# An attention-and-experts block on one core: its middle stage written anew, with input summed in place and other orders of loads and stores

## The chip, the cores and the metric

One Trainium2 chip, one of its cores. The time is device microseconds (us) of one execution of the whole program, the median of three runs; it holds the launch's own device work beside the span that the profile shows. A measurement of this kernel tells changes of about 0.3% from none.

## The reference

Input x is 8 sequences of 1024 tokens of width 256. In float32:

```
x = x + attention(layernorm(x))          # 16 heads of width 16, rotary, keys = values
                                         # out @ Wout + bout
y = layernorm(x)
scores = softmax(y @ gate_w.T)           # 8 experts
vals, idx = top_k(scores.T, 1024)        # each expert takes 1024 of the 8192 tokens
z = layernorm(y[idx]) * ln_w + ln_b
h = gelu(z @ fc1.T + b1);  o = (h @ fc2.T + b2) * vals
x = x + (y with o added at the rows idx)
```

## The kernel before, in words

The program has five stages, and three of them stand in one block of instructions (`project_attend_finish`, L1867): *project* (layer norm, the projections, rotary), *attend* (64 pairs of heads), and *finish*. Behind it come *choose* (L1297, the top-k by counting) and *experts* (L1451), each in a block of its own; all engines meet at the end of a block before the next begins. The change is to finish, and to where its first and last transfers stand.

Finish (L869) goes over 64 tiles of 128 tokens, eight to a sequence, two sequences to a pass of 16 tiles. Per tile, with the tile index counted from 0:

- PE multiplies the attended rows by Wout (`project_tile`, L1228) in two chunks of 128 rows, and adds the bias by a third product of a few bfloat16 rows (L1238), into one of two banks of PSUM.
- DVE adds the tile of x (`residual`, L1055) into a buffer of its own, `x2`, takes its mean and variance (`statistics`, L1065; POOL takes the inverse root, L1022), and writes the normalised tile `xf` (L1076). It does the statistics of `xf` as well, for the second layer norm.
- The value that goes to `out` is x2 + xf (`base`: POOL for three tiles in four at L1035, DVE for the fourth at L1084).
- PE turns `xf` round (`turn`, L1240), ACT copies it (L1169), PE multiplies it by the gate weights (`logits`, L1248). Here the gate weights (8 columns) are the stationary operand and 128 tokens stream, so the logits come with experts in rows. For each group of four tiles ACT copies them (`turned_logits`, L1186) and PE turns them back by four products with the identity (`turn_back`, L1261).
- ACT writes the row of the token table (`normalise_again`, L1176); DVE and ACT do the softmax once per sequence (`centre`, `exponential`, `share`, `scores`).

Each engine runs a table of lags: in step j it does stage S for tile j - lag (L877), 16 steps to a pass. The first two passes are written out, the next two are a loop, and a tail follows.

The loads and stores of finish are all issued by SP, in one order that is written by hand (`sync`, L980). SP waits in order, so a load that waits for an engine holds back every store behind it. Its body, per pass:

```
load_o(it + 1, 0)                 # waits until PE is done with that half of o
store_tab(it - 1, 0); store_out(it - 1, 1)
load_x(it + 1, 0)
load_o(it + 1, 1)                 # the same wait, for the other half
store_tab(it - 1, 1); store_out(it, 0)
load_x(it + 1, 1)
```

`x2` holds two sequences, so `residual` of a sequence waits until the store of the sequence two before has landed (L1061). `load_o` waits also for the attended rows on their way to DRAM (`attended`, L583), of all sequences once past the first pass.

The last pairs of attend are not complete when finish begins: the reciprocals and products of the last two pairs are done between the tiles of finish (`invert_last` at DVE's step 6, `scale_second` at POOL's step 6, `scale_last` at its step 12; L1900, L1913). SP issues finish's constants and its first loads (`load_first`, L971) within attend's last pairs (L646). The constants are used by DVE at the start of finish: it splits the bias into three bfloat16 parts (`split_bias`, L1116), and PE waits for that (L1286).

At the end of finish SP waits for all stores (L1017 to L1019), and with it every engine at the end of the block. Choose then loads its four constants (L1346).

Of the kernel before, what the change touches and what calls it, by code (L numbers as in the profile page):

```python
# [868 lines left out]
def finish(nc, ctx, own, x, on_dram, w_out, b_out, w_gate, ident_d, table, out, gate):  # L869


    SEQS = 2
    STEP = SEQS * TILES
    PASSES = B // SEQS
# [16 lines left out]
    o = mem.sb("f_o", [P, SEQS, DC, N])  # L891
    xb = mem.sb("f_x", [P, STEP, D])
    x2 = mem.sb("f_x2", [P, STEP, D])
    xf = mem.sb("f_xf", [P, STEP, D])
    tab = mem.sb("f_tab", [P, STEP, ROW])
    stats = mem.sb("f_stats", [P, 2, STEP, 6])
    mv = mem.sb("f_mv", [P, 2, STEP, 2])
    veps = mem.sb("f_veps", [P, 2, STEP])
    rstd = mem.sb("f_rstd", [P, 2, STEP])
    shift = mem.sb("f_shift", [P, STEP])  # L900
    xfT = mem.sb("f_xfT", [P, 2, DC, P])
    lT = mem.sb("f_lT", [E, 2, LGROUP * P])
# [5 lines left out]
    ps_y = mem.ps("f_ps_y", [P, 2, 512])  # L908
    ps_xT = mem.ps("f_ps_xT", [P, 2, 4, P])
    ps_lT = mem.ps("f_ps_lT", [P, 2, LGROUP * P])  # L910
    ps_l = mem.ps("f_ps_l", [P, 2, 512])

    consts_in = a.sem("f_consts_in")
    set_up = a.sem("f_set_up")
    o_in = [a.sem(f"f_o_in{s}") for s in range(SEQS)]
    x_in = [a.sem(f"f_x_in{s}") for s in range(SEQS)]
    out_out = [a.sem(f"f_out_out{s}") for s in range(SEQS)]
    tab_out = [a.sem(f"f_tab_out{s}") for s in range(SEQS)]
    bias_done = a.sem("f_bias_done")
# [11 lines left out]
    lT_done = a.sem("f_lT_done")  # L931
    back_done = a.sem("f_back_done")
# [16 lines left out]
    flow = Flow(STEP, PASSES)  # L949

    def one(v):
        return bass.ds(v, 1)

    def tiles_of(s):
        return slice(s * TILES, (s + 1) * TILES)

    def load_o(sp, attended, it, s):
        if past(it):

            sp.wait_ge(y_done, it * STEP + (s + 1 - SEQS) * TILES)  # L960
        attended(sp, B if past(it) else s + 1)
        sp.dma_start(o[:, s], o_v[one(it * SEQS + s)].rearrange("o p c n -> p (o c) n")).then_inc(o_in[s], 16)

    def load_x(sp, it, s):
        if past(it):

            sp.wait_ge(x2_done, it * STEP + (s + 1 - SEQS) * TILES)
        sp.dma_start(xb[:, tiles_of(s)], x_v[one(it * SEQS + s)].rearrange("o p i d -> p (o i) d")
                     ).then_inc(x_in[s], 16)

    def load_first(sp, attended):  # L971
        sp.dma_start(bo[:], b_out.rearrange("(o n) -> o n", o=1).to_broadcast([PARTS, D])).then_inc(consts_in, 16)
        sp.dma_start(ident[:], ident_d).then_inc(consts_in, 16)
        sp.dma_start(w[:], w_out.rearrange("(c p) n -> p c n", p=P)).then_inc(consts_in, 16)
        sp.dma_start(wg[:], w_gate).then_inc(consts_in, 16)
        for s in range(SEQS):
            load_o(sp, attended, 0, s)
            load_x(sp, 0, s)

    def sync(sp, attended):  # L980
# [13 lines left out]
        def body(it):  # L994

            load_o(sp, attended, it + 1, 0)
            if past(it):
                store_tab(it - 1, 0)
                store_out(it - 1, 1)
# [994 lines left out]
```

## Time and profile before

| | us |
|---|---|
| median of three runs | 2326.22 |
| lowest, highest | 2322.04, 2328.96 |
| the profiled execution's own time | 2336.65 |
| its span in the profile | 2333.8 |
| finish, first product to last share of the softmax | 1603.97 to 1818.47 |
| waits of DVE's residual in finish for a store to land | 51.3, in 5 waits |

Whole-span busy time: PE 2072.6 (89%), DVE 1951.5 (84%), ACT 1511.4 (65%), POOL 648.8 (28%). Read it with care: these are averages over five stages, and finish is 9% of the span. Engine names: PE is TensorE, PEld its weight loads, DVE VectorE, ACT ScalarE, POOL GpSimd, SP the queue that issues transfers. "Granted clock" is TensorE's, as a share of full speed. In the timeline a row is a start, a duration (of several instructions together where it says x2 or more), the engine, the line, what is written from what, and in brackets how long the engine sat idle before it and what released it.

### The profile page before, as it was taken

How to read it: one execution, taken by the hardware profiler on the slowest of the kernel's cores; microseconds unless marked ns; L12 is line 12 of the kernel's file. 1: busy time of each engine (PE TensorE's matmuls, PEld its weight loads, DVE VectorE, ACT ScalarE, POOL GpSimd, SP SyncE). 2: the span in 40 equal slices, each digit the busy share in tenths (PEclk: the TensorE clock that was granted, in tenths of full speed). 3: DMA queues.
4: the chain of work that ended last, by engine and by line, in shares of the span. 5: the costliest groups of instructions: out<-in, count | busy, mean ns of one | idle time of the engine just before them, and what ended most of it. 6: DMA issues, size and time to landing. Idle time of an engine off the chain costs nothing. (4 is left out here: it accounts for less than half of the span.)

```text
span 2333.8 us, 53856 instructions
## 1 busy us (share of the span) xinstructions
PE 2072.6 (89%) x16812; PEld 1055.1 (45%) x16812; DVE 1951.5 (84%) x3220; ACT 1511.4 (65%) x2858; POOL 648.8 (28%) x864
## 2 busy tenths in 40 slices
PE   6777699999999999999999999999768218999998
PEld 3334233333333333333333333334445117998997
DVE  7888789999999999999999999994546667988864
ACT  3444278888888888888888888884223103455433
POOL 7788101110111110111111011112435013655553
PEclk9999589999999999999999999999879558999999
DMA  3667624444334344333444434433444122343342
GB/s 96 217 222 201 185 54 82 80 81 80 77 73 78 81 79 82 76 74 75 82 79 82 78 75 74 80 67 120 155 146 145 59 74 72 83 101 84 86 83 29
DMA packets 152669, 224.66 MB, mean 96 GB/s; under 512 B 34855, under 2 KB 105098, under 8 KB 152586
## 3 DMA queue, kind: packets, MB, share of 16 engines
q1 hardware_dynamic: 140262, 206.61, 36.7%
q0 software_dynamic: 12288, 17.05, 4.4%
q8 instruction: 38, 0.62, 0.1%
q14 instruction: 45, 0.37, 0.1%
q10 hardware_dynamic: 36, 0.02, 0.0%
HBM read 129.45 MB, written 93.06 MB: 95 GB/s over the span
## 5 line engine op out<-in xcount | busy, mean ns | idle before, releaser
L761 DVE TENSOR_REDUCE a_mx<-a_sm 128x2 f32<-128x1024 f32 x1024 | 1235.6, 1224 | 70.1 <-PE a_sm L709 54.2
L836 ACT ACTIVATE a_prob<-a_st 128x512 f32<-128x512 f32 x2048 | 1113.6, 597 | 180.0 <-PE a_st L672 149.2
L709 PE MATMUL a_sm<-a_k,a_q 48*128 48x512 f32 x2048 | 759.2, 460 | 9.3 <-DVE a_mx L761 7.6
L672 PE MATMUL a_st<-a_q,a_k 50*128 50x512 f32 x2048 | 761.2, 452 | 5.8 <-DMA a_q<-a_mrow 5.8
L696 PE MATMUL a_pv<-a_prob,a_v 128*32 128x256 f32 x8192 | 660.7, 394 | 23.0 <-ACT a_oraw L843 22.4
L672 PEld LDWEIGHTS a_st<-a_q,a_k 50*128 50x128 f32 x2048 | 312.8, 187 | 415.1 <-ACT a_prob L836 395.5
L696 PEld LDWEIGHTS a_pv<-a_prob,a_v 128*32 128x32 f32 x8192 | 162.2, 108 | 404.9 <-issue 198.5
L811 POOL TENSOR_TENSOR a_v<-a_v_raw,a_zero 128x256 f32<-128x256 f32 x64 | 39.7, 622 | 1049.1 <-DMA a_v_raw<-values 900.6
L709 PEld LDWEIGHTS a_sm<-a_k,a_q 48*128 48x128 f32 x2048 | 306.3, 189 | 21.2 <-DVE a_mx L761 19.2
L1779 ACT ACTIVATE e_hT<-e_ps_h,e_b1b 128x512 f32<-128x512 f32 x128 | 88.3, 690 | 213.3 <-PE e_ps_h L1816 203.0
L1816 PE MATMUL e_ps_o<-e_w_high,e_hT_high 128*128 128x256 f32 x512 | 146.9, 287 | 2.8 <-DVE e_biased L1681 2.8
L1816 PE MATMUL e_ps_o<-e_w_low,e_hT_high 128*128 128x256 f32 x512 | 145.4, 284 | 0.0
L1816 PE MATMUL e_ps_o<-e_w_high,e_hT_low 128*128 128x256 f32 x512 | 145.3, 284 | 0.0
L381 PE MATMUL p_ps_q<-p_w,p_xnT 128*128 128x512 f32 x256 | 127.0, 620 | 0.0
L1732 POOL TENSOR_TENSOR e_ahead<-e_row_no 128x1 f32<-128x1 f32 x72 | 49.6, 689 | 266.9 <-DVE e_idx L1625 173.5
L1669 DVE TENSOR_TENSOR e_hT_low<-e_hT,e_hT_high 128x512 fp32r<-128x512 f32 x128 | 86.8, 692 | 42.9 <-ACT e_hT_high L1785 38.5
L1755 POOL DMA_INDIRECT out_dram<-e_ob,e_idx x64 | 110.0, 1719 | 13.7 <-issue 8.4
L1816 PE MATMUL e_ps_h<-e_yT_high,e_w_high 128*128 128x512 f32 x256 | 101.8, 398 | 0.4 <-ACT e_hT L1779 0.4
L1816 PE MATMUL e_ps_h<-e_yT_low,e_w_high 128*128 128x512 f32 x256 | 100.9, 394 | 0.0
L1816 PE MATMUL e_ps_h<-e_yT_high,e_w_low 128*128 128x512 f32 x256 | 100.7, 393 | 0.0
L1816 PEld LDWEIGHTS e_ps_o<-e_w_high,e_hT_high 128*128 128x128 f32 x512 | 98.8, 193 | 3.4 <-DVE e_biased L1681 3.0
L307 POOL TENSOR_TENSOR p_tsin<-p_qkv,p_sin 128x256 f32<-128x256 f32 x128 | 98.3, 788 | 3.7 <-ACT p_qkv L345 3.7
(148 smaller groups left out, 2354.0 us busy)
## 6 DMA issues: line engine op xcount, KB each, us to landing
qkv_parts<-p_parts SPq DMA_DIRECT2D x64, 512.0 KB
a_q<-qkv_parts SPq DMA_DIRECT2D x128, 128.0 KB, 3.5
a_k<-qkv_parts SPq DMA_DIRECT2D x128, 128.0 KB, 4.3
attended<-a_oraw SPq DMA_DIRECT2D x64, 256.0 KB, 3.8
e_w<-in_fc_dram SPq DMA_DIRECT2D x16, 1024.0 KB, 5.4
token_table<-f_tab SPq DMA_DIRECT2D x8, 1056.0 KB, 7.1
p_x<-in_x_dram SPq DMA_DIRECT2D x16, 512.0 KB, 8.1
values<-p_values SPq DMA_DIRECT2D x8, 1024.0 KB, 19.6
```

The lines of the kernel that those rows point to most:

```text
L307: nc.gpsimd.tensor_tensor(ts[:, :, h * HALF:(h + 1) * HALF], src[:, :, (1 - h) * HALF:(2 - h) * HALF], sinb[:, i:i + 1, h * HALF:(h + 1) * ...
L381: mm = nc.tensor.matmul(ps_q[:, k % 2], xnT[:, k % 2, c], w[:, c], start=(c == 0), stop=(c == DC - 1))
L672: nc.tensor.matmul(st[:, slot % RING], kb[rows, q.buf, jt * P:(jt + 1) * P], qb[rows, q.buf, ic * CHUNK:(ic + 1) * CHUNK], start=True, sto ...
L696: mm = nc.tensor.matmul(pv[row:row + 2 * DH, cols], vb[:, q.buf, jt, h, :], prob[:, jt % 2, h, start:start + QUARTER], start=(jt == 0 and ...
L709: mm = nc.tensor.matmul(sm[:, slot, h], qb[rows, q.buf, qt * P:(qt + 1) * P], kb[rows, q.buf, kc * CHUNK:(kc + 1) * CHUNK], start=True, st ...
L761: nc.vector.tensor_reduce(mx[:, qt, kc, :], sm[:, slot], AX.X, ALU.max, negate=True).then_inc(max_done, 1)
L836: nc.scalar.activation(prob[:, jt % 2, h, ic * CHUNK:(ic + 1) * CHUNK], st[:, slot % RING], ACT.Exp, scale=DH ** -0.5).then_inc(drained, 1)
L1669: nc.vector.tensor_tensor(group_of(hT_low, g), hT[:, g % 4], group_of(hT_high, g), ALU.subtract).then_inc(hT_low_done, 1)
L1732: nc.gpsimd.tensor_tensor(ahead[:], row_no[:], row_no[:], ALU.add).then_inc(ahead_done, 1)
L1755: nc.gpsimd.indirect_dma_start(out=out_rows, out_offset=bass.IndirectOffsetOnAxis(ap=idx[:, k, i:i + 1], axis=0), in_=ob[:, i], in_offset= ...
L1779: nc.scalar.activation(hT[:, g % 4], ps_h[:, g % 3], ACT.Gelu_apprx_tanh, bias=b1b[:, k, g % FC:g % FC + 1]).then_inc(gelu_done, 1)
L1816: return nc.tensor.matmul(to, weights, moving, start=first, stop=last)
```

## The change

Finish is written out for all 64 tiles, without a loop, in a new form:

- `xb` holds four sequences instead of two, and `residual` and `base` write into it: `x2` is gone. `load_x` of sequence s waits for the store of sequence s - 4.
- `residual` waits for no store. PE has three banks for the output product instead of two.
- SP's order per sequence s: load o of s + 2, store the table of s - 1, load x of s + 3, store out of s. `load_first` loads x of four sequences instead of two. `load_o` of sequence s waits for the attended rows of sequences up to s only. The last sequence's stores go in halves.
- The logits: 128 tokens are the stationary operand, the 8 columns of the gate weights stream. The result has tokens in rows; `turned_logits`, `turn_back` and their banks are gone.
- The bias product uses all 128 rows: `ones` and `bo_rows` have 128 partitions, rows 3 to 127 of `bo_rows` are zero.
- The constants of finish are loaded and the bias split ahead of project's work (`Early`); Wout and the gate weights are loaded between project and attend.
- SP's waits for the stores of finish stand in the block of choose, behind the loads of its constants (`finished`).
- All lags are three less: the late steps go from 6, 6, 12 to 3, 3, 9, the same tiles as before.

```diff
-    PROJ, STAT, NORM, TURN, LOGITS, SHIFT, NORM2, BACK, CENTRE, SHARE = 3, 4, 7, 8, 9, 10, 11, 11, 12, 13
+    STAT, NORM, TURN, LOGITS, SHIFT, NORM2, CENTRE, SHARE = 1, 4, 5, 6, 7, 8, 9, 10
...
+    OSEQS, XSEQS, TSEQS = 2, 4, 2
+    YBANKS = 3
...
+        self.bo_rows = mem.sb("f_bo_rows", [P, D], BF16)
+        self.ones = mem.sb("f_ones", [P, P], BF16)
...
+    def load_o(sp, attended, s):
+        if s >= OSEQS:
+
+            sp.wait_ge(y_done, (s + 1 - OSEQS) * TILES)
+        attended(sp, s + 1)
+        sp.dma_start(o[:, s % OSEQS], o_v[s]).then_inc(o_in[s % OSEQS], 16)
+
+    def load_x(sp, s):
+        if s >= XSEQS:
+
+            sp.wait_ge(out_out[s % XSEQS], 16 * (s // XSEQS))
+        sp.dma_start(xb[:, ring(s, XSEQS)], x_v[s]).then_inc(x_in[s % XSEQS], 16)
...
+        for s in range(B):
+            if s + OSEQS < B:
+                load_o(sp, attended, s + OSEQS)
+            if s > 0:
+                store_tab(s - 1, 0, s * TILES)
+            if XSEQS <= s + XSEQS - 1 < B:
+                load_x(sp, s + XSEQS - 1)
+            if s < B - 1:
+                store_out(s, 0, (s + 1) * TILES)
...
-                if past(it):
-
-                    dve.wait_ge(out_out[s], 16 * it)
             dve.wait_ge(y_done, n + 1)
-            nc.vector.tensor_tensor(x2[:, k], ps_y[:, k % 2, 0:D], xb[:, k], ALU.add).then_inc(x2_done, 1)
+            nc.vector.tensor_tensor(xb[:, n % XRING], ps_y[:, n % YBANKS, 0:D], xb[:, n % XRING], ALU.add
+                                    ).then_inc(x2_done, 1)
...
-                mm = nc.tensor.matmul(ps_lT[0:E, (k // LGROUP) % 2, i * P:(i + 1) * P], wg[:, c], xfT[:, k % 2, c],
+                mm = nc.tensor.matmul(ps_l[:, s % 2, i * E:(i + 1) * E], xfT[:, n % 2, c], wg[:, c],
                                       start=(c == 0), stop=(c == DC - 1))
...
             for buf, name in ((ident, "ident"), (same, "same"), (before, "before"), (bits, "bits")):
                 sp.dma_start(buf[:], consts[name]).then_inc(consts_in, 16)
+            finished(sp)
...
+            early.load_bias(sp, t["b_out"], t["ident"])
             first.sync(sp, load_pairs)
+            early.load(sp, t["w_out"], t["w_gate"])
             second.sync(sp, stored, load_finish)
...
         def _(dve):
+            early.split_bias(dve)
             first.vector(dve)
             second.vector(dve)
-            third.vector(dve, {6: invert_last})
+            third.vector(dve, {3: invert_last})
```

PE's instructions for tiles in the middle of finish, before: output product, bias, turn, logits, and every fourth tile the turn back.

```order
L1236 MATMUL f_ps_y<-f_w,f_o 128x256 x2
L1238 MATMUL f_ps_y<-f_bo_rows,f_ones 128x256
L1245 MATMUL f_ps_xT<-f_ident,f_xf 128x128 x2
L1257 MATMUL f_ps_lT<-f_xfT,f_wg 8x128 x2
L1270 MATMUL f_ps_l<-f_ident,f_lT 128x8 x4
```

And of the change, at the same place:

```order
L1231 MATMUL f_ps_y<-f_w,f_o 128x256 x2
L1233 MATMUL f_ps_y<-f_bo_rows,f_ones 128x256
L1240 MATMUL f_ps_xT<-f_ident,f_xf 128x128 x2
L1251 MATMUL f_ps_l<-f_wg,f_xfT 128x8 x2
L1231 MATMUL f_ps_y<-f_w,f_o 128x256 x2
```

The logits product writes 128 rows of 8 instead of 8 rows of 128, and the four products of the turn back are gone.

SP's queue within attend's last pairs, before (`a_den`, `a_num` are the denominators and numerators that come back for a pair, L612 the store of its reciprocals):

```order
L607 DMA a_num<-attended 64x1x512
L972 DMA f_bo<-in_b_out_dram 3x256
L973 DMA f_ident<-in_ident_dram 128x128
L974 DMA f_w<-in_w_out_dram 128x2x256
L975 DMA f_wg<-in_w_gate_dram 128x16
L962 DMA f_o<-attended_normalised 128x2x1024
L968 DMA f_x<-in_x_dram 128x8x256
L962 DMA f_o<-attended_normalised 128x2x1024
L968 DMA f_x<-in_x_dram 128x8x256
L612 DMA reciprocal_denominators<-a_rden 128x16
```

And of the change:

```order
L607 DMA a_num<-attended 64x1x512
L1002 DMA f_o<-attended_normalised 128x2x1024
L1008 DMA f_x<-in_x_dram 128x8x256
L1002 DMA f_o<-attended_normalised 128x2x1024
L1008 DMA f_x<-in_x_dram 128x8x256 x3
L612 DMA reciprocal_denominators<-a_rden 128x16
```

Four small loads are gone from here, and two loads of x (1 MB each) have come in front of L612.

## Rows read from the trace of the kernel before

**Rows 1.** Busy time in stretches: us, engines' busy (count), granted clock, DMA share, GB/s.

```profile
1776.00:1804.00 28.00, 28.00 (x153) 17.16 (x152) 21.00 (x93) 12.07 (x29) 17.24 (x32) 1.00 0.37 126
...
1827.00:1890.00 63.00, 11.31 (x39) 9.44 (x40) 44.63 (x146) 0.00 (x0) 0.00 (x0) 0.50 0.00 0
```

**Rows 2.** Waits of 1550 to 1950 us: who waited, for whom, total us, times, longest.

```profile
DVE f_x L1063 <- DMA out_dram<-f_x: 51.3, 5, 11.5
```

**Rows 3.** Timeline, DVE, residual of tiles 3, 48 and 63: start, us, instruction, idle before.

```profile
1612.13 0.42 DVE L1063 TENSOR_TENSOR f_x<-f_ps_y,f_x 128x256 f32<-128x256 f32 x1
...
1768.70 0.42 DVE L1063 TENSOR_TENSOR f_x<-f_ps_y,f_x 128x256 f32<-128x256 f32 x1 [10.89 <-DMA out_dram<-f_x]
...
1805.51 0.42 DVE L1063 TENSOR_TENSOR f_x<-f_ps_y,f_x 128x256 f32<-128x256 f32 x1 [0.17 <-PE f_ps_y L1238]
```

**Rows 4.** Timeline, PE, one tile at full clock and the group's turn back behind it.

```profile
1755.03 1.13 PE L1236 MATMUL f_ps_y<-f_w,f_o 128*128 128x256 f32 x4
...
1756.09 0.28 PE L1238 MATMUL f_ps_y<-f_bo_rows,f_ones 3*128 3x256 bf16 x1
...
1756.30 0.44 PE L1245 MATMUL f_ps_xT<-f_ident,f_xf 128*128 128x128 f32 x2
...
1756.66 0.60 PE L1257 MATMUL f_ps_lT<-f_xfT,f_wg 128*8 128x128 f32 x4
...
1757.20 1.05 PE L1270 MATMUL f_ps_l<-f_ident,f_lT 8*128 8x8 f32 x8
...
1758.18 1.13 PE L1236 MATMUL f_ps_y<-f_w,f_o 128*128 128x256 f32 x4
```

**Rows 5.** Timeline, DVE, residuals of tiles 8, 10 and 50.

```profile
1620.77 0.42 DVE L1063 TENSOR_TENSOR f_x<-f_ps_y,f_x 128x256 f32<-128x256 f32 x1 [0.83 <-PE f_ps_y L1238]
...
1625.05 0.42 DVE L1063 TENSOR_TENSOR f_x<-f_ps_y,f_x 128x256 f32<-128x256 f32 x1 [0.60 <-PE f_ps_y L1238]
...
1774.16 0.42 DVE L1063 TENSOR_TENSOR f_x<-f_ps_y,f_x 128x256 f32<-128x256 f32 x1 [0.37 <-PE f_ps_y L1238]
```

**Rows 6.** Timeline, SP queue, the store of sequence 4.

```profile
1758.17 0.40 SPq L984 DMA_DIRECT2D out_dram<-f_x  x1
```

**Rows 7.** Busy time in three-microsecond stretches, columns as in rows 1.

```profile
1637.00:1640.00 3.00, 3.00 (x20) 2.06 (x18) 1.31 (x4) 1.14 (x3) 2.16 (x4) 1.00 1.02 237
...
1763.00:1766.00 3.00, 0.00 (x0) 0.00 (x0) 0.00 (x0) 0.00 (x0) 0.00 (x0) 0.67 1.09 361
```

**Rows 8.** Timeline, PE, the output product just after a stall.

```profile
1744.04 2.08 PE L1236 MATMUL f_ps_y<-f_w,f_o 128*128 128x256 f32 x4
```

**Rows 9.** Timeline, SP queue, from attention's last pairs to the finish.

```profile
1578.07 0.47 SPq L972 DMA_DIRECT2D f_bo<-in_b_out_dram  x1
...
1583.66 4.21 SPq L612 DMA_DIRECT2D reciprocal_denominators<-a_rden  x1
...
1595.63 0.60 SPq L616 DMA_DIRECT2D a_rrep<-reciprocal_denominators  x1
...
1603.85 0.60 SPq L605 DMA_DIRECT2D a_den<-attended  x1
```

**Rows 10.** Timeline, DVE and PE at the same place.

```profile
1599.50 0.25 DVE L563 RECIPROCAL a_rden<-a_den 128x16 f32<-128x16 f32 x1 [20.31 <-DMA a_den<-attended]
...
1603.97 2.05 PE L1236 MATMUL f_ps_y<-f_w,f_o 128*128 128x256 f32 x4 [4.24 <-DVE f_bo_rows L1131]
```

**Rows 11.** Timeline, from the last logits to the choice of tokens.

```profile
1815.25 0.56 ACT L1192 COPY f_lT<-f_ps_lT 8x512 f32<-8x512 f32 x1
...
1816.96 0.23 DVE L1100 TENSOR_REDUCE f_lmax<-f_ps_l 128x8 f32<-128x64 f32 x1 [1.13 <-PE f_ps_l L1270]
...
1818.87 0.37 SPq L991 DMA_DIRECT2D token_table<-f_tab  x1
...
1827.39 1.12 PE L1355 MATMUL c_ps_t<-c_ident,c_by_group 128*128 128x128 f32 x4 [10.47 <-DMA c_bits<-in_bits_dram]
```

**Rows 12.** Timeline, DVE, the program's first statistics.

```profile
6.86 1.41 DVE L231 BATCH_NORM_STATS2 p_stats<-p_x 128x6 f32<-128x256 f32 x4 [5.94 <-DMA p_sin<-in_rot_sin_dram]
```

More of the change, by code:

```diff
@@ new lines, in steps, with tile, ring @@
+    def steps(body, last_lag):
+        for j in range(TILES_ALL + last_lag):
+            body(j)
+    def tile(j, lag):
+        return j - lag if 0 <= j - lag < TILES_ALL else None
+    def ring(s, seqs):
+        return slice((s % seqs) * TILES, (s % seqs + 1) * TILES)
+    def load_o(sp, attended, s):
[7 more added lines that the diff above has]
+        sp.dma_start(xb[:, ring(s, XSEQS)], x_v[s]).then_inc(x_in[s % XSEQS], 16)
@@ L1220, in body @@
+        def body(j):
+            n = tile(j, TURN)
+            if n is not None:
+                turned(n)
+            n = tile(j, NORM2)
+            if n is not None:
+                normalise_again(n)
             for stage, lag in ((exponential, CENTRE), (scores, SHARE)):
-                tile = flow.at(it, j, lag)
-                if tile and tile[1] % TILES == TILES - 1:
-                    stage(*tile)
-        flow.run(act, body, SHARE)
+                n = tile(j, lag)
+                if n is not None and n % TILES == TILES - 1:
+                    stage(n // TILES)
@@ L1274, in body @@
-        def body(it, j):
-            for stage, lag in ((project_tile, PROJ), (turn, TURN), (logits, LOGITS)):
-                tile = flow.at(it, j, lag)
-                if tile:
-                    stage(*tile)
-            tile = flow.at(it, j, BACK)
-            if tile and tile[1] % LGROUP == LGROUP - 1:
-                turn_back(*tile)
-        banks_left(pe)
-        pe.wait_ge(consts_in, 64)
-        pe.wait_ge(set_up, 3)
-        pe.wait_ge(bias_done, 3 * PARTS)
-        flow.run(pe, body, BACK)
@@ L1289, in finish, with body @@
-    return Stage(sync, tensor, vector, scalar, gpsimd), load_first
+        def body(j):
+            for stage, lag in ((project_tile, 0), (turn, TURN), (logits, LOGITS)):
+                n = tile(j, lag)
+                if n is not None:
+                    stage(n)
+        banks_left(pe)
+        pe.wait_ge(early.consts_in, 32)
+        pe.wait_ge(early.bias_done, 3 * PARTS)
+        steps(body, LOGITS)
+    return Stage(sync, tensor, vector, scalar, gpsimd), load_first, stored
 ROUNDS = 15
@@ L1294, with choose @@
 UNROLL = 5
[L1297 removed]
+def choose(nc, gate, consts, places_hi, places_lo, finished):
     GROUP = TOK // 16
@@ L1876, in project_attend_finish @@
                                                 parts, values)
-        third, load_next = finish(nc, ctx, ctx, t["x"], on, t["w_out"], t["b_out"], t["w_gate"], t["ident"], table, out,
-                                  gate)
+        third, load_next, finished = finish(nc, ctx, ctx, early, stores, t["x"], on, table, out, gate)
         block = ctx.enter_context(nc.Block())
```

453 lines of the change are left out of this document (200 added, 253 removed).

## The prediction

> **What bounds the kernel now.** I read the rows of the page first (busy shares, the slices with the granted clock), and since the change touches one stage of five, then the stretch of that stage: first its waits, then the timeline of DVE, PE and SP around one wait. Finish is a pipeline of 64 tiles. Where it runs freely PE sets its pace: in 28 us PE is busy for all 28, DVE for 21, ACT for 12, POOL for 17, at the full clock [rows 1]. One tile costs PE 1.06 us for the output product, 0.21 for the bias, 0.36 for the turn and 0.54 for the logits (from start to start), and each group of four 0.98 more for the turn back [rows 4]: 2.17 + 0.245 = 2.415 us a tile. But tiles 3 to 63 took 1805.51 - 1612.13 = 193.4 us [rows 3], which is 3.22 a tile. The largest part of the difference is one wait: DVE's residual waits 51.3 us in five pieces for the store of `out` [rows 2]. The one at tile 48 took 10.89 [rows 3]: SP issued the store it needed only at 1758.17 [rows 6], since the load of o, which waits until PE is through the next sequence, stood ahead of it. While it lasts PE idles, the granted clock falls (0.67 in the mean of that stretch) [rows 7], and the first output product behind such a wait takes 2.08 us [rows 8] where it takes 1.13 at the full clock [rows 4]. That is the level of 1.2 GHz beside that of 2.4.
>
> **The steady tiles.** In the change the residual waits for no store. The store of sequence s now holds back only x of sequence s + 4, which SP issues some 15 tiles before it is used. So all five waits go, and with them the slow tiles behind each. What is late next is PE. Its logits become four passes (two chunks, two passes each in the count x4) that load 128 columns and stream 8. The trace has that form in the turn back: eight passes in 0.98 us, 0.1225 each [rows 4], with 8 rows in place of 128. So the logits cost 0.49 in place of 0.54, the turn back nothing, and a tile 1.06 + 0.21 + 0.36 + 0.49 = 2.12 us. The bounds are 2.12, and 2.42 where the 128-row weights eat what the turn back gave. I take the low end, as its row has the same columns loaded and streamed.
>
> The Trainium skill ("TensorE: Matmul & The Clock Gate", Part 3) has a rule against this: a weight load overlaps a running matmul only when the row groups differ, and by its section on LDWEIGHTS a load of 128 columns lasts P / 1.2 ns, some 107 ns, with the contraction rows of no account. By it new and old logits passes would cost about the same (a long load and a short stream for the reverse), and the tile 2.17, 3 us more over 60 tiles. The rows say that the overlap is partly there: four output passes of 256 columns take 1.06 us [rows 4].
>
> DVE must keep up. From tile 8 to tile 10 it takes 1625.05 - 1620.77 less 0.60 of waiting = 3.68 us for two tiles [rows 5]. In the two steps with the softmax it takes 1774.16 - 1768.70 less 0.37 = 5.09 [rows 3, 5], 1.4 more, once in eight tiles: 1.84 + 0.18 = 2.02 a tile. The change adds and takes nothing there. That is near PE's 2.12, and the third bank lets PE run over DVE's uneven steps, so I take 2.15. Sixty tiles then take 129.0 us in place of 193.4: **-64.4**.
>
> The transfers need room: per sequence 1 MB each of o, x and out and 1.06 MB of table (1 MB is 1.049 million bytes) make 4.3 million bytes, in 8 x 2.15 = 17.2 us, 248 GB/s. The queues did 361 in a stretch full of them, and 237 in the worst mixed one at the same full share [rows 7]. At 361 there is a third to spare; 237 is a rival below.
>
> **The handover.** Before, DVE takes the second-last pair's reciprocal at 1599.50, after 20.31 us of waiting, splits the bias, and PE waits 4.24 us for that until 1603.97 [rows 10]. The split goes. But SP's queue is what holds that reciprocal back: the loads start at 1578.07, L612 behind them needs 4.21 us to be issued, its data lands at about 1595.6 when L616 follows, and then the denominators are fetched [rows 9]. The change takes four small issues away (2 us earlier) and adds 2.1 million bytes of x ahead of L612; at 361 GB/s that is 5.8 us, net some 4 us. So I expect L616 at 1599.7, the reciprocal at 1603.5 and the first residual at 1603.9. The last pair's denominators, fetched at 1603.85 before [rows 9], are fetched some 4 us later and land at 1610.5, where DVE stands before tile 3 waiting for them (it did not wait there before). Tile 3's residual comes at 1610.8 against 1612.13: **-1.3**. PE, three tiles ahead, idles for some 4 us meanwhile. For the slow tiles after that I add **+2.0** (two output products at 2.08 in place of 1.13). Queued behind DVE's wait are residuals 3 onward, then POOL's roots and PE's turns. The pieces have bounds: -3.7 (no added delay), and +8 (the loads delay twice over, as the last pair has two trips through the queue).
>
> **The end of finish.** From ACT's copy of the logits at 1815.25 to DVE's maximum at 1816.96 [rows 11] lie just the copy and the turn back: **-1.7**. From the last table store at 1818.87 to choose's first product at 1827.39 are 8.5 us [rows 11]: the store lands, all engines meet, four constants load. Now the meeting does not wait for the landing, but the constants queue behind the stores (2 MB in the last microseconds) and land about when these do. I take 5.5 us: **-3.0**, bounds 0 and -5.
>
> **The program's start.** Two issues stand ahead of project's loads, about 0.45 us each by the issue times of such loads [rows 9]. The bias split, 4.24 us at most [rows 10], runs on DVE while it waits for project's constants until 6.86 [rows 12]. I take **+0.9**, bounds 0 and +4.2. The load of Wout between project and attend I cost at nothing: no engine waits for it for 1200 us, and SP then waits for stores anyway. Written-out tiles in place of a loop are costed at nothing; tiles 3 to 31 were written out before.
>
> **The sum.** -64.4 - 1.3 + 2.0 - 1.7 - 3.0 + 0.9 = -67.5 us. On the profiled execution that is 2336.65 - 67.5 = 2269.2. That execution lies 10.4 above the median of the runs, 2326.22; from the median the sum gives **2258.7 us**.
>
> **The rivals.**
>
> *Transfers take over as the bound.* At the mixed 237 GB/s a sequence needs 18.1 us, 2.27 a tile (+7), and if out or table land late on top, table buffers come free late and ACT waits: one wait of 2 us a sequence, 16 more. That gives 2266 to 2282. For it: 1.02 share at 237 GB/s, and that transfers now run beside work all the time. Against: o is loaded some nine tiles ahead, x fifteen. 12%.
>
> *The store's wait comes back elsewhere.* The waits go through SP, which is still one queue in order: if it stands behind a load of o as before, the table store of s - 1 or x of s + 3 is late, and each sequence waits for 6 to 10 us again. Then only PE's 0.3 a tile (17 us) and the ends (3 us) remain: 2306. Against: by the lags the store of out is issued as soon as it is ready, twelve steps after the sequence's first tile, and x has four buffers. 5%.
>
> *Slower: the clock does not rise.* Products that stream 8 columns replace some that stream 128; choose, whose products stream 1 to 3, sits at 0.50 with PE busy 11.3 of 63 us [rows 1]. If finish ran at 1.2 GHz throughout, a tile would cost 2.12 x 2.08 / 1.13 = 3.9 us, 60 of them 234, 41 more than before; with the other terms the end is 2362. It decides from 3.3 us a tile upward. Against: the output product is half of PE's time and is untouched, and PE would have hardly a gap, whereas in choose it mostly waits. 3%.
>
> **How the numbers follow.** Forecast 80%: 2258.7, and its bounds are 2250 (2.12 a tile, no delay at the handover, the boundary at -5) to 2275 (2.42 a tile, or handover and start both at their worst). To reach 8 in 10 of all cases the range takes in most of the transfers' rival: 2249 to 2284. A measurement tells about 0.3%, 7 us, from no change. Faster by more: the forecast and the first two rivals, 0.96 with a rest left out; slower 0.03; same 0.01.
>
> **What would show it.** Right: no wait of the residual for `out`; residuals 2.1 to 2.2 us apart in mid-stage; the granted clock at 1.00 from about tile 8 to 63; logits passes 0.12 apart; one wait of about 4 us for `a_den` before tile 3; choose's first product some 5.5 us after the last table store. Wrong: PE waiting for o, ACT's table waiting for its store, residuals 2.4 or more apart with PE not busy (DVE's or POOL's pace, which I took for 2.02), or a clock under 0.9 in mid-stage.

## The result and the profile after

The changed kernel takes 2246.24 us (median; 2240.46 to 2249.00), the kernel before 2326.27 beside it: a ratio of 0.9654, 95% interval 0.963 to 0.9678, 80.0 us less. The forecast was 2258.7, its range began at 2249.0: the direction was right, the gain was undersized by 12.5 us. The profiled execution took 2246.26 us, at the median.

I measure the stage by one stretch: from the fetch of the third-last pair's numerators (L607, the row ahead of finish's loads; the expectations below call it the last pair but one's) to choose's first product. It is 249.94 us before, 167.76 after, 82.2 less. The parts are the handover up to tile 3's residual, 34.68 us before and 35.91 after; tiles 3 to 63, 193.38 and 113.03; and from tile 63 to choose, 21.88 and 18.82. The program's start costs 0.92. Project and attention are the same within 2 us. The profiled execution of before spent 6.3 us more behind choose's first product, where the change has no part.

DVE's residuals after, in the columns of [rows 3]:

```profile
1612.24 0.25 DVE L563 RECIPROCAL a_rden<-a_den 128x16 f32<-128x16 f32 x1 [6.51 <-DMA a_den<-attended]
1612.41 0.36 DVE L1093 TENSOR_TENSOR f_x<-f_ps_y,f_x 128x256 f32<-128x256 f32 x1
...
1621.48 0.42 DVE L1093 TENSOR_TENSOR f_x<-f_ps_y,f_x 128x256 f32<-128x256 f32 x1
...
1636.13 0.42 DVE L1093 TENSOR_TENSOR f_x<-f_ps_y,f_x 128x256 f32<-128x256 f32 x1 [0.48 <-PE f_ps_y L1233]
...
1725.44 0.42 DVE L1093 TENSOR_TENSOR f_x<-f_ps_y,f_x 128x256 f32<-128x256 f32 x1
```

These are the last pair's reciprocal and tiles 3, 8, 16 and 63. No tile waits for a store. The 60 intervals are 1.88 us each in the mean. Now the stretches, in the columns of [rows 1], and the waits from 1600 to 1740 us, which answer to [rows 2]:

```profile
1605.00:1610.00 5.00, 2.37 (x13) 1.59 (x11) 0.69 (x5) 0.00 (x0) 1.53 (x3) 1.00 0.26 94
1610.00:1615.00 5.00, 0.60 (x3) 0.60 (x4) 2.72 (x12) 0.00 (x0) 1.43 (x3) 0.73 0.19 63
1615.00:1620.00 5.00, 5.00 (x22) 4.13 (x21) 2.77 (x14) 0.76 (x3) 2.58 (x6) 0.59 0.10 33
...
1650.00:1670.00 20.00, 18.41 (x116) 14.79 (x115) 19.23 (x88) 9.60 (x25) 16.13 (x32) 1.00 0.88 300
```

```profile
PEld f_ps_xT L1240 <- DVE f_xf L1113: 30.0, 46, 7.4
...
DVE f_x L1093 <- PE f_ps_y L1233: 2.6, 3, 1.4
```

In mid-stage DVE is busy 19.23 of 20 us, and it waits for PE three times in the stage, 2.6 us in all; PE's weight loads wait for DVE 46 times. The bound has passed from PE to DVE. The reason is PE's tile, which answers to [rows 4]:

```profile
1620.15 1.11 PE L1231 MATMUL f_ps_y<-f_w,f_o 128*128 128x256 f32 x4
1621.10 0.27 PE L1233 MATMUL f_ps_y<-f_bo_rows,f_ones 128*128 128x256 bf16 x1
1621.21 0.38 PE L1240 MATMUL f_ps_xT<-f_ident,f_xf 128*128 128x128 f32 x2
1621.42 0.51 PE L1251 MATMUL f_ps_l<-f_wg,f_xfT 128*128 128x8 f32 x4
1621.79 1.11 PE L1231 MATMUL f_ps_y<-f_w,f_o 128*128 128x256 f32 x4
```

From start to start: product 0.95, bias 0.11, turn 0.21, logits 0.37, together 1.64 us, where I had 2.12. The weight loads (LDWEIGHTS) show why. First the kernel before, PE's loads around one bias product (which ran at 1620.39), then after (ran at 1621.10):

```profile
1620.38 0.09 PEld L1238 LDWEIGHTS f_ps_y<-f_bo_rows,f_ones 3*128 3x128 bf16 x1 [0.33 <-issue]
1620.59 0.20 PEld L1245 LDWEIGHTS f_ps_xT<-f_ident,f_xf 128*128 128x128 f32 x2
1620.96 0.32 PEld L1257 LDWEIGHTS f_ps_lT<-f_xfT,f_wg 128*8 128x8 f32 x4 [0.17 <-issue]
1621.50 0.19 PEld L1236 LDWEIGHTS f_ps_y<-f_w,f_o 128*128 128x128 f32 x1 [0.22 <-issue]
```

```profile
1620.88 0.10 PEld L1233 LDWEIGHTS f_ps_y<-f_bo_rows,f_ones 128*128 128x128 bf16 x1
1621.10 0.25 PEld L1240 LDWEIGHTS f_ps_xT<-f_ident,f_xf 128*128 128x128 f32 x2
1621.32 0.53 PEld L1251 LDWEIGHTS f_ps_l<-f_wg,f_xfT 128*128 128x128 f32 x4
```

The 3-row load started with its own product, after 0.33 us of nothing, and loads at a change to or from 8 columns stood 0.17 and 0.22 us. Where every load is 128 by 128, the bias's starts 0.22 us ahead of its product, while the product before still runs, and no gap is left.

At the handover and at the end (SP's queue, then DVE and PE), answering to [rows 9] and [rows 11]:

```profile
1579.11 10.36 SPq L1008 DMA_DIRECT2D f_x<-in_x_dram  x3
1589.51 3.23 SPq L612 DMA_DIRECT2D reciprocal_denominators<-a_rden  x1
...
1607.45 0.60 SPq L605 DMA_DIRECT2D a_den<-attended  x1
...
1738.41 0.92 SPq L1036 DMA_DIRECT2D token_table<-f_tab  x2
```

```profile
1744.26 1.11 PE L1333 MATMUL c_ps_t<-c_ident,c_by_group 128*128 128x128 f32 x4 [9.31 <-DMA c_bits<-in_bits_dram]
```

### The profile page after: what moved, and what is told of

Its sections match the earlier page's. It is cut to its first block and busy times, and to the rows that moved or that the text cites. A ratio compares the mean times of both kernels' runs of the same rounds, so it can differ in the third digit from the quotient of the medians.

```text
span 2244.4 us, 53244 instructions
## 1 busy us (share of the span) xinstructions
PE 2011.2 (90%) x16684; PEld 1046.1 (47%) x16684; DVE 1947.5 (87%) x3221; ACT 1503.5 (67%) x2842; POOL 648.3 (29%) x864
## 5 line engine op out<-in xcount | busy, mean ns | idle before, releaser
L1647 DVE TENSOR_TENSOR e_hT_low<-e_hT,e_hT_high 128x512 fp32r<-128x512 f32 x128 | 86.4, 689 | 40.5 <-ACT e_hT_high L1763 40.5
L1794 PE MATMUL e_ps_h<-e_yT_high,e_w_low 128*128 128x512 f32 x256 | 100.8, 394 | 0.0
L345 ACT COPY p_qkv<-p_ps_q 128x512 f32<-128x512 f32 x64 | 37.5, 586 | 94.4 <-PE p_ps_q L381 54.6
```

What stands on the lines that cost most here:

```text
L1647: nc.vector.tensor_tensor(group_of(hT_low, g), hT[:, g % 4], group_of(hT_high, g), ALU.subtract).then_inc(hT_low_done, 1)
L1794: return nc.tensor.matmul(to, weights, moving, start=first, stop=last)
```

## The experiments

All times are medians, beside the kernel before on the same chip, whose median was 2322 to 2334 from chip to chip. The difference to it, and the stretch from L607 to choose's product in the profiled execution, are therefore the better measures; the stretch is that of one execution. e5 and e6 have none, since their edit moves loads ahead of L607. "Clock" says how the stage ran in the profile.

| run | edit | us | to before | stretch | clock |
|---|---|---|---|---|---|
| after | | 2246.2 | -80.0 | 167.8 | falls at the handover, returns |
| e1 | 3-row bias | 2332.2* | +4* | 258.6 | 1.2 from tile 3 to the end |
| e2 | 32-row bias | 2331.4* | +3* | 258.4 | the same |
| e3 | before, 128-row bias | 2317.8 | -10.3 | 240.0 | falls at each wait, returns |
| e4 | before, new logits | 2352.1 | +23.9 | 278.1 | 1.2 from the first store wait |
| e5 | first loads a pair earlier | 2249.2 | -85.2 | | 1.2 in attention's last pair |
| e6 | e5 and 3-row bias | 2260.3* | -74.1* | | returns (one of four: not) |
| e7 | before, both | 2305.0 | -29.4 | 224.2 | as e3 |
| e8 | all bases on POOL | 2237.5 | -96.9 | 164.9 | as after |
| e9 | x of third, fourth later | 2238.7 | -86.4 | 169.3 | falls there and at tile 16, returns |
| e10 | two PSUM banks | 2241.8 | -83.3 | 167.5 | as after |
| e11 | ring of two sequences | 2288.7 | -36.4 | 218.4 | as e3 |
| e12 | e8 and e9 | 2238.6 | -86.5 | 165.2 | falls at tile 16, returns |
| e13 | loads by need | 2238.3 | -84.1 | 164.7 | the same |
| e14 | e13 and e8 | 2234.2 | -88.2 | 160.5 | the same |
| e15 | e13 and 3-row bias | 2309.0 | -13.4 | 237.2 | 1.2 from tile 16 |
| e16 | e14, third's loads earlier | 2232.5 | -99.9 | 158.1 | as after, shorter |
| e17 | after again | 2243.4 | -89.0 | 168.1 | as after |
| e18 | e16 and 3-row bias | 2238.6* | -94* | 252.6 | 1.2 in the profiled one |

(*) Executions of e1, e2, e6 and e18 fall into two groups far apart, told below; a profile shows one of them.

**Which of PE's two edits counts.**

```diff
-            nc.tensor.matmul(ps_y[:, n % YBANKS, 0:D], ones[:], bo_rows[:], start=False, stop=True)
+            nc.tensor.matmul(ps_y[:, n % YBANKS, 0:D], ones[0:PARTS], bo_rows[0:PARTS], start=False, stop=True)
```

> The kernel after with the bias product over 3 rows again (ones 3x128, bias 3x384), all else as after. Theory 1 (the 128-row bias lets TensorE take the next weights ahead; 3 rows cost issue gaps before and behind the product): of the 0.78 us that TensorE's unstalled tile lost, bias, turn and product carry 0.10 + 0.15 + 0.11 = 0.36, so the tile goes from 1.64 to about 2.00 us, above VectorE's 1.89, and 60 tiles cost 60 x 0.11 = 6.6 us: 2249 to 2256 us. Rival A (the form of the logits alone made TensorE faster, rows of the bias are of no account): tile stays 1.64 to 1.70, time within 0.5 us of after (2246). Rival B (the 3-row load costs more than in the kernel before, since no turn-back work is there to cover it): tile 2.2 or more, 2262 or more.

> As the run before, with the bias over 32 rows. If the load is held up because it uses another height of the array than the products around it, whatever that height: TensorE's tile as with 3 rows (about 2.00 us by theory 1), 2249 to 2256 us. If it is only the very small row count (3) that is slow: tile near 1.64, time 2246. Rival A expects no change in either run.

(The second has 32 for PARTS.) No theory held. Nine of ten executions of e1 took 2328.6 to 2340.9 us with a mean clock of 0.909 to 0.915, one took 2242.2 with 0.956; e2 has the same nine (2325 to 2346) and one (2244.5). No profile shows one of the two short ones. The profile of e1, in stretches, and one tile of it:

```profile
1610.00:1615.00 5.00, 1.94 (x9) 0.92 (x7) 0.00 (x0) 0.00 (x0) 1.97 (x2) 0.89 0.17 55
1615.00:1620.00 5.00, 1.65 (x5) 1.48 (x6) 3.38 (x13) 0.37 (x1) 1.70 (x3) 0.50 0.16 57
...
1650.00:1670.00 20.00, 20.00 (x63) 13.68 (x63) 10.54 (x48) 5.66 (x14) 8.99 (x17) 0.50 0.50 159
...
1790.00:1810.00 20.00, 20.00 (x63) 13.67 (x63) 10.54 (x48) 5.66 (x14) 8.98 (x17) 0.50 0.16 55
```

```profile
1702.69 2.05 PE L1231 MATMUL f_ps_y<-f_w,f_o 128*128 128x256 f32 x4
1704.68 0.39 PE L1233 MATMUL f_ps_y<-f_bo_rows,f_ones 3*128 3x256 bf16 x1
1705.00 0.69 PE L1240 MATMUL f_ps_xT<-f_ident,f_xf 128*128 128x128 f32 x2
1705.48 0.86 PE L1251 MATMUL f_ps_l<-f_wg,f_xfT 128*128 128x8 f32 x4
1706.19 1.20 PE L1231 MATMUL f_ps_y<-f_w,f_o 128*128 128x256 f32 x2
```

PE idles 6.4 us at the handover (7.0 in the kernel after), and its clock falls to 1.2 GHz, as there. But there it is back at 2.4 after two slow tiles. Here PE is busy 20.00 of 20 us for 190 us and it never returns; a tile takes 3.50. The two halves alone, added to the kernel before:

> The kernel before with only the bias over 128 rows (zeros below the three). Theory 1: TensorE's unstalled tile 2.415 less 0.36 = 2.05 us; where TensorE was the bound (about 3 us of the 60 tiles' mean 3.22 each cannot all be, the five waits for the output's stores of 10 us stay) 0.36 x 60 = 21.6 us at most, so 2304 to 2314 us. Rival A (form of the logits alone): no change, 2325 to 2328. Rival C (transfers set the pace of the kernel before, so a faster TensorE only waits longer at the stores): TensorE's tile 2.05, but time down by less than 5 us, and the waits for the stores grow by what is gained.

> The kernel before with only the new logits (token columns as the stationary side, no turn back, no copy on ScalarE). Theory 1: it takes the turn back's 0.245 and the logits' 0.17 us, tile 2.415 to 2.00 us, 2300 to 2314 us. Rival A: all of the 0.78 us come from here, tile 1.64, 2285 to 2300 us. Rival C: TensorE's tile shorter, time down by less than 5 us.

> The kernel before with both changes of TensorE's work (bias over 128 rows, new logits), rings, orders, loads and stores as before. Theory 3: the clock comes back after each wait as with the 128-row bias alone; TensorE's unstalled tile 1.64, so VectorE's 1.89 sets the pace in place of 2.17 plus the turn back 0.245: 0.5 us x 60 = 30 us less what the five waits for stores and the slow clock behind each eat (the 128-row bias alone gave 10 of 15): 2300 to 2310 us; the rest of the 80 us, 55 to 65, then belongs to the rings and orders of the transfers. Rival H (TensorE's work is most of the gain): 2275 us or less. Rival I (clock stays at 1.2 GHz after the first wait): 2340 to 2355 us.

e3, then e4, one tile each at 2.4 GHz:

```profile
1619.26 1.13 PE L1238 MATMUL f_ps_y<-f_w,f_o 128*128 128x256 f32 x4
1620.23 0.27 PE L1240 MATMUL f_ps_y<-f_bo_rows,f_ones 128*128 128x256 bf16 x1
1620.34 0.38 PE L1247 MATMUL f_ps_xT<-f_ident,f_xf 128*128 128x128 f32 x2
1620.65 0.60 PE L1259 MATMUL f_ps_lT<-f_xfT,f_wg 128*8 128x128 f32 x4
1621.18 1.13 PE L1238 MATMUL f_ps_y<-f_w,f_o 128*128 128x256 f32 x4
```

```profile
1617.12 1.11 PE L1222 MATMUL f_ps_y<-f_w,f_o 128*128 128x256 f32 x4
1618.16 0.28 PE L1224 MATMUL f_ps_y<-f_bo_rows,f_ones 3*128 3x256 bf16 x1
1618.37 0.44 PE L1231 MATMUL f_ps_xT<-f_ident,f_xf 128*128 128x128 f32 x2
1618.64 0.51 PE L1242 MATMUL f_ps_l<-f_wg,f_xfT 128*128 128x8 f32 x4
1619.01 1.11 PE L1222 MATMUL f_ps_y<-f_w,f_o 128*128 128x256 f32 x4
```

The sizes add up: 2.17 without the turn back becomes 1.92 by the 128-row bias (0.25 less) and 1.89 by the new logits (0.28 less, beside 0.245 of turn back), and 1.64 by both. e3 gained 10.3 us (ratio 0.9926, 0.9896 to 0.9955), short of theory 1's 12 to 22 (it had 0.36 a tile). e4 became slower (1.0085, 1.0066 to 1.0104), which no theory foresaw, and its clock tells why: after the first store wait, at 1.2 GHz,

```profile
1640.00:1650.00 10.00, 9.35 (x31) 7.07 (x32) 7.38 (x35) 3.59 (x9) 5.75 (x11) 0.50 0.02 8
...
1750.00:1770.00 20.00, 20.00 (x64) 13.69 (x62) 9.24 (x40) 5.16 (x11) 8.75 (x16) 0.50 0.12 35
```

it is at 0.50 to the end of the stage. e7 came out at 2305.0 (0.9895, 0.9846 to 0.9944), inside its 2300 to 2310: both edits on PE are worth 25.8 us of the stretch; the other 56.4 belong to rings, orders and boundary. That is the share when PE's edits come first, with the store waits in place; no run has the new rings and orders without them. So of four mixes (3 or 128 rows, old or new logits) only one stayed slow for a whole stage after a fall: 3 rows with the new logits. The 128-row bias is what lets the new logits be used.

**Is idle time the cause of the fall?** e5 and e6 issue the finish's first loads a pair earlier (`if q.p == NP - 3`):

> The kernel after with the finish's first loads (two o, four x, 6 MB) issued one pair earlier, at the pair before the one that issued them. Theory 2 (the 10.36 us in which SyncE's queue stood at the x loads made the last pair's denominators late, and with them tile 3; TensorE idled 7 us and its clock fell to 1.2 GHz for two tiles): the 6.5 us wait for a_den before the last inversion shrinks to under 3 us, tile 3 comes 3 to 6 us earlier, the clock stays 1.00 through the first tiles: 2238 to 2243 us. Rival E (the chain of the last pair's own small transfers sets tile 3, whatever is loaded): wait of 5 us or more, 2245 to 2247 us. Rival F (the loads now collide with the last pair's row of maxima, TensorE waits there instead): a new wait of 3 us or more at a_q<-a_mrow, 2246 us or more.

> As the run before, and the bias over 3 rows. Theory 3, formed after the runs with 3 and 32 rows: rows of the bias cost no time as such (TensorE's tile 1.89 us at 2.4 GHz, no more than VectorE's), but with the new logits and a 3-row bias a clock that has once fallen to 1.2 GHz does not rise again in this stage (tile 3.50 us, profile 2339); with 128 rows it rises. So if TensorE no longer idles before tile 3 and the clock stays up: 2238 to 2246 us with the granted clock at 1.00 and TensorE's tile at 1.89 us; if the idle time and the fall remain: 2325 to 2340 us. Rival G (3 rows pull the clock down by themselves, without an idle time ahead): clock 0.5 from a place without idle time, over 2300 us.

Rival F won in e5. The 6 MB stood ahead of the last pair's maxima, PE waited 4.5 us for `a_q<-a_mrow`, and its clock fell in mid-attention. It stayed down to the end of attention, 33 us in which PE was nearly always busy, and rose at the first tiles of finish:

```profile
1560.00:1577.00 17.00, 12.48 (x115) 4.74 (x107) 3.99 (x5) 11.51 (x23) 1.20 (x3) 0.98 0.77 253
...
1587.00:1600.00 13.00, 13.00 (x80) 3.80 (x80) 0.27 (x3) 7.82 (x16) 1.26 (x1) 0.50 0.03 8
```

In e6 the clock was low too, rose at 1617 us while PE ran products of the first tiles without turns, and three of four executions took 2255 to 2260, one 2342.5. In its profile the 3-row mix ran mid-stage at 1.00, PE's tile 1.90 us and the pace 1.96: 3 rows by themselves cost 0.08 a tile, at the new logits and 2.4 GHz. The better handovers told more. Loads by need (e13): x of sequences two and three leave the first batch, and go behind the o of the same sequence:

```diff
         for s in range(B):
             if s + OSEQS < B:
                 load_o(sp, attended, s + OSEQS)
+            if OSEQS + s < XSEQS:
+                load_x(sp, OSEQS + s)
```

> The kernel of the first of these three with the bias over 3 rows. Theory 3: with the shorter handover TensorE idles for 3 us in place of 7 (the run with x later had 3.2), and where its clock does not fall, the whole stage runs at 2.4 GHz: the stretch 168 to 172 us (TensorE's 1.90 and the gaps of a 3-row load: 1.96 to 1.98 us a tile as in the run with earlier loads), the kernel 2243 to 2252. Where the clock falls at the handover it stays at 1.2 GHz to the end of the stage: stretch over 250, kernel 2325 to 2340. Both may be seen among the executions, nothing between. Rival G (3 rows slow the stage at 2.4 GHz too, or let the clock fall without idle time): executions between 2255 and 2320.

> The first of these three with the bias over 3 rows. Theory 3 as it stands now (the 3-row mix costs 0.25 us of TensorE a tile and nothing else at 2.4 GHz; only an idle time of TensorE lets the clock fall, and in this mix a fall in mid-stage lasts to its end): with no wait of over 3 us at tile 16 the stage stays at 1.00 to the last tiles, TensorE's 1.90 us is the pace: 154 + 60 x 0.1 = 160 us of stretch, 158 to 164, kernel 2230 to 2240. If the fall comes without an idle time, at some tile in mid-stage: stretch 180 to 250 us, kernel over 2255. If it falls at the handover's wait and stays: stretch over 240.

e15 (2302.9 to 2312.7) fell between the groups, where theory 3 had expected nothing and rival G its 2255 to 2320. Its profile bears out neither of rival G's reasons: at 2.4 GHz tiles 8 to 15 take 0.06 us each more than in after, and the fall comes behind idle time.

```profile
1615.00:1620.00 5.00, 5.00 (x32) 3.57 (x30) 4.68 (x19) 2.63 (x7) 4.84 (x9) 1.00 0.10 16
...
1630.00:1640.00 10.00, 8.88 (x32) 6.34 (x32) 7.71 (x36) 3.49 (x9) 5.81 (x11) 0.61 0.93 310
1640.00:1650.00 10.00, 10.00 (x33) 7.14 (x33) 5.60 (x27) 2.40 (x6) 3.56 (x8) 0.50 0.60 205
```

It passed the handover: 1.66 us of idle time, one tile at 1.2 GHz, then back, so a short fall can be undone in this mix, which theory 3 had ruled out. It ran at 2.4 up to tile 16, met a gap of 4.5 us between residuals 15 and 16 (PE itself idled 2.23), and stayed at 1.2 from there. With that wait gone too (e18), four of five executions took 2233.8 to 2240.5, about what theory 3 gave, and one, the profiled one, 2322.6: PE waited 1.73 us for `f_xf`, and from the second product behind that (1603.68) all take 2.05 us. So a 3-row kernel can run as fast as after, and its time is a lottery: one short execution in ten in e1 and in e2, none in seven in e15, four in five in e18. In the profiles of e1, e2, e15 and e18 idle time of PE stands ahead of the fall; that their short executions had less of it is not shown, since no profile shows one. Idle time is not enough, either. At the same place, with the 128-row bias, e13 kept its clock through 3.16 us where e9 lost it after 3.18:

```profile
1596.32 0.44 PE L1240 MATMUL f_ps_xT<-f_ident,f_xf 128*128 128x128 f32 x2 [3.16 <-DVE f_xf L1113]
```

That the 128-row mix undoes a fall is shown in e9, where it came back twice. What the chip weighs in a mix, these runs do not show.

**What bounds the tile now.** e8 sums x and normalised x of every tile on POOL (`if n is not None: base(n)`, DVE's part and its semaphore out of the store's wait); e10 has `YBANKS = 2`:

> The kernel after with the sum x + normalised x of every tile on GpSimd (before: three of four, the fourth on VectorE, 393 ns each). Theory 1 in its part on the bound (VectorE's 1.89 us a tile sets the pace, TensorE has 1.64, GpSimd 75 of 98 us busy): VectorE 1.79, GpSimd 1.69 a tile, 60 x 0.1 = 6 us: 2239 to 2242 us. Rival J (the pace comes from the chain between engines or from transfers, DMA 0.84 busy): 2245 to 2248 us. Rival K (GpSimd's inverse roots come late behind the sums and VectorE waits for them): over 2249 us.

> The kernel after with two PSUM banks for the projected tile, not three. Theory 1: VectorE is busy all the time and TensorE (1.64 of 1.89 us) waits for it in either case, so no change in the steady tiles; 2245 to 2249 us. Rival L (the third bank is what lets TensorE run ahead and so keeps VectorE fed): VectorE's wait for f_ps_y grows from 2.6 us to over 10, 2252 us or more.

e8 cut the steady pace from 1.89 to 1.83 (14.63 us for eight tiles, 15.13 in after) and the stretch by 2.9 us, half of the 6 forecast. DVE's sum had taken 0.39 us, but 0.31 from start to start, which is 0.08 a tile and not 0.1. Where the rest went is not shown: DVE is still busy 38.71 of 40 us, and POOL, at 35.97, has little room left. The span of its profiled execution is 100.8 us under before's, and 7.9 of that lie ahead of the stretch, 7.8 behind it, where the edit has no part. e10 changed nothing in the stretch (167.5), though its median is under the 2245 to 2249 expected: the third bank is not needed at DVE's pace.

**The rings.**

> The kernel after with the ring of x cut from four sequences to two (the load of a sequence's x then waits for the store of the one two before; it stands ahead of the table's store in the queue). Theory 1 in its part on the stalls (the five waits of 10 us for the output's stores made 51 of the 80 us, with the slow clock behind them): an output's store is issued 9.6 us behind its sequence's last residual and takes 6 us, the load of x 6 to 7, so a sequence takes 22 to 24 us in place of 15.1, six times: 2290 to 2310 us, with the clock at 0.5 to 0.9 behind each wait. Rival M (something else of the new order, not the ring, removed the waits): under 2270 us.

```profile
DVE f_x L1093 <- DMA f_x<-in_x_dram: 41.2, 6, 8.3
```

With `XSEQS = 2` (and the load of x ahead of the table's store) six waits of some 7 us return, now for the load of x, and the stretch grows by 50.6 us. From tile 3 to 63 it is 56.0, since with 4 MB of first loads the handover is 5.4 shorter. The time, 2288.7, is just under the theory's 2290. The ring of four sequences, with its place in the order, is the largest single part of the change.

**The handover, and a better version.**

> The kernel after with the loads of x of the third and fourth sequence (2 of 6 MB) issued behind the last pair's chain, not ahead of it. Theory 2 (SyncE's queue stood 10.36 us at the x loads and the last pair's denominators came late by that): the wait for a_den before the last inversion, 6.5 us, shrinks by 3 to 6 us, tile 3 comes that much earlier, and TensorE, idle for less, may keep 2.4 GHz: 2239 to 2243 us. Rival E (the chain of small transfers sets tile 3 whatever is loaded): wait 5 us or more, 2244 to 2248 us.

> Both of: all bases on GpSimd (ran 2237.5 us, its steady tiles 1.83 in place of 1.89 us) and x of the third and fourth sequence loaded later. If the two are independent, as theories 1 and 2 say: 5 us less than after for the one and 3 to 6 for the other, 2234 to 2239 us, and no more than the slower of the two if the later loads bring nothing.

> The kernel after with x of the third and fourth sequence loaded behind the last pair's chain, each behind the o of the same sequence. From the issue of the last pair but one's numerators to the choice's first product the kernel after took 167.8 us, the run with both x loads ahead of that o 169.3 (handover 5.5 us shorter, but a wait of 6.5 us for o and slow tiles behind it). Theory 2: the handover keeps its 30.4 us (after: 35.9) and the wait at tile 16 is gone or under 2 us, so the stretch takes 162 to 164 us, the kernel 2238 to 2243. Rival E: 166 us or more.

> The same with all bases on GpSimd (that alone: 164.9 us for the stretch). The two are independent by theories 1 and 2: 167.8 - 2.9 - 5 = 160 us, 158 to 162; the kernel 2230 to 2240. If GpSimd, at 1.69 of 1.83 us a tile, holds up the last pair's scaling: 163 us or more.

> As the run with loads by need and all bases on GpSimd (stretch from the last pair's numerators to the choice's first product 160.5 us), and o and x of the third sequence issued ahead of the last pair's final write. The 5.2 us between tiles 15 and 16 and the three slow tiles behind it (3.2 in place of 1.83 us each) go: 160.5 - 3.4 - 3 = 154 us, 153 to 157, granted clock 1.00 from tile 4 to the last: kernel 2226 to 2232. If the transfers now collide with the last pair's chain: 160 us or more.

> The kernel after itself, on the same chip as the run before it: 2240 to 2249 us, stretch 167 to 169 us; the difference to the run before it 10 to 15 us by theory 2, and under 8 if the gains of the orders were differences between executions.

e9's wait for `a_den` shrank from 6.51 to 2.86 us and L607 to tile 3 from 35.91 to 30.43: the two last loads of x ahead of L612 were the cause. Whether by SP's standing at them or by the transfers themselves, no run separates. But its stretch did not shrink (169.3), since o of the third sequence now stood behind the moved loads:

```profile
1636.90 2.08 PE L1232 MATMUL f_ps_y<-f_w,f_o 128*128 128x256 f32 x4 [6.49 <-DMA f_o<-attended_normalised]
```

The median of 2238.7 alone would have been read as a gain of the edit. The profiled execution, with 2249.5 the slowest of the five, shows none in the stretch, and e10, with the stretch of after, took 2241.8 on the same chip. e12 has the same wait (10.2 us between residuals 15 and 16). e13 puts o first: 164.7 (162 to 164 expected), with 1.45 us of waiting for o and 5.3 between residuals 15 and 16; e14 160.5, inside its range. e16 issues x and o of the third sequence ahead of the last pair's final write, and the wait at tile 16 is gone: 158.1 us, median 2232.5 (ratio 0.9584, 0.9545 to 0.9624) against 2243.4 of after on the same chip (0.9629, 0.9588 to 0.9671). By the stretches it is 10.0 us faster than after, less than the 14 expected. Against e14 the wait at tile 16 gave 3.8 us back, but the clock fell behind the 3.08 us wait for `f_xf` at tile 3, where e14's had not: tiles 3 to 8 took 8.45 us, not 6.80. The 3 us expected from the slow tiles at tile 16 were not there to gain: from tile 16 to 63 e14 took 86.4 us and e16 86.3.

## Why the prediction was right and wrong

**The steady tiles, -64.4 forecast, -80.4 measured.** This term was mis-sized, and it carries the whole miss. That all five store waits go with the slow tiles behind them was right (e11 brings waits back, and 50.6 us). The step that failed is the pace of 2.15 us a tile, and both figures under it. The first is "a tile 1.06 + 0.21 + 0.36 + 0.49 = 2.12 us" for PE, measured 1.64. It took the times from start to start of three parts from [rows 4] as if they belonged to the instruction; part of each was the gap at a change of shape: product 0.95, bias 0.11, turn 0.21. The 128-row bias I costed at nothing; it takes 0.25 off a tile (e3). For the logits I took 0.1225 a pass from the turn back, the row with the same columns; that row has 8-row loads and its gaps, and the new pass costs 0.09.

The second figure, DVE's 2.02, was 1.89: eight tiles take 15.13 us. The 1.4 us for the softmax was right. The 1.84 without it was not: the two tiles of [rows 5] hold one of the sums that DVE takes only for every fourth tile, so I counted half a sum a tile and not a quarter:

```profile
1622.65 0.39 DVE L1086 TENSOR_TENSOR f_x<-f_x,f_xf 128x256 f32<-128x256 f32 x1
```

The same two tiles take 3.59 us in the kernel after, where 3.68 was read; the mean without softmax is 1.72 a tile. With PE at 1.64, DVE's is the term that counts: 60 x (2.15 - 1.88) = 16 us, half of it from PE's figure (2.15 to 2.02) and half from DVE's. The sum of the terms as measured, with the slow tiles inside the first, is -80.4 + 1.2 - 3.1 + 0.9 = -81.4, beside -80.0 in the medians. By the terms, tiles 3 to 63 came out 18.0 us under the forecast (-62.4 with the slow tiles), and the handover and the end together 4.1 over it.

**The Trainium skill's rule** ("TensorE: Matmul & The Clock Gate", Part 3), that a load overlaps a running product only when the row groups differ, gave 2.17 in the prediction's estimate. Here the rows show such an overlap without that condition: between products of the same 128 rows the load started 0.22 us ahead of its product, the 3-row load not at all. The measurement decides.

**The handover, -1.3 and +2.0 forecast.** Tile 3 came 1.2 us later after L607, not 1.3 earlier: DVE's wait for `a_den` was 6.5 us, forecast 4. The cause I gave, more loads of x ahead of L612, is confirmed (e9). Its delay was about right: the last pair's denominators were fetched 4.55 us later after L607 than before, forecast some 4. What was mis-sized is their way: I let them land 2.65 us behind the fetch (1607.85 to 1610.5), and DVE took them 4.8 us behind it (1607.45 to 1612.24), in e9 as well. The +2.0 for the slow tiles was right: PE idled 7 us, its clock fell, and tiles 3 to 8 took 9.07 us. In e5, e12, e13 and e14, where the clock stood at 1.00 from tile 3 on, they took 6.80, so the fall cost 2.3.

**The end and the start.** The maximum comes 1.0 us earlier after tile 63 (forecast 1.7), and from it to choose's product 2.1 (forecast 3.0). From the issue of the last two table stores to that product are 5.85 us, forecast 5.5. The start costs 0.92, forecast 0.9.

**The rivals.** Transfers did not bound: they did 300 GB/s at a share of 0.88 beside full work, above the 237 that I had feared, and in mid-stage no engine waited for them by more than 0.3 us. No store wait came back. The slower rival named the right danger for a wrong reason: not the logits' 8 columns alone, but these with the 3-row bias, keep the clock down (e1, e4). Its 3.9 us a tile was 3.50, and its 2362 was 2332. In the kernel after, the bias's zero rows bar that way, which I had not seen: the rows of zeros were an edit that I costed at nothing, and without them nine executions in ten of e1 came out near the rival's time.

**What would show it.** Right: no waits for `out`, the clock at 1.00 in mid-stage, a wait for `a_den` before tile 3, if of 6.5 us and not 4. Wrong: residuals 1.9 apart, not 2.1 to 2.2; logits passes 0.09, not 0.12; a "pace of DVE's", which I had listed as a sign of being wrong upward and which came out downward.

## What to carry over

A start-to-start time in a full queue holds the gaps at changes of shape; before adding such times up for a new mix, look at the weight loads and at what ended the gap ahead of each. Where work falls unevenly on tiles, take a whole cycle of them as the sample: here eight, not two. Find the next bound at its own full pace, not at the pace of the engine that held it back. And where the clock falls in a stage, ask which mix of work will have to bring it back: an edit that saves PE 0.5 us a tile made a kernel 24 us slower, and 125 rows of zeros turned it into a gain. Judge edits worth under 1% by the stretch of the trace that they touch: the kernel after itself stood 80 and 89 us below before on two chips, while its stretch agreed within 0.4 us. The stretch is read from one execution, though: see first where that one stands among the others.

## What the runs showed of the hardware

After an idle time of PE the granted clock can fall from 2.4 to 1.2 GHz. It had fallen after 1.45 us (e13, at tile 16) and after 7.0 (after), but stood through 1.82 (e5, 1616.75) and 3.16 (e13, 1596.32). PE being busy does not bring it back by itself: 20.00 of 20 us busy at 0.50, for 190 us (e1), 13.00 of 13 in attention (e5). With a 128-row bias the same stage brings it back in two or three tiles (after, e9, e13). Where it fell at the handover, that cost 1.6 to 2.8 us (tiles 3 to 8: 8.45 to 9.64 us in e9, e16, after and e17, and 6.80 where it stood). At 1.2 GHz a tile of the 3-row mix takes 3.50 us, of the 128-row mix 3.22 (e9, 1636.90 to 1640.12). At 2.4 GHz a bfloat16 load of 128 by 128 starts 0.22 us ahead of its own product, while the product before still runs; at loads with 3 rows, or at a change to or from 8 columns, the load queue stood 0.17 to 0.33 us. Three issues of x loads of SP's, behind three other loads, took 10.36 us, and the small one after them 3.23. The denominators of a pair (8 KB) were used by a waiting DVE 4.8 us after their fetch was issued (after, e9).
